# Four tokens in a row on each partition, one transfer for a token shift, fewer half-blocks on GpSimd, and a new order of steps

## The reference, cut to what matters

```
def shift_token(t):
    t1, t2 = jnp.split(t, 2, axis=-1)
    t2 = jnp.pad(t2, ((0, 0), (1, 0), (0, 0)))[:, :-1]
    return jnp.concatenate([t1, t2], axis=-1)
```

```
h = shift_token(x);  q, k, v = split(h @ wqkv)     # 8 heads of 64, windows of 64 tokens
q, k = rotary(l2norm(q)), rotary(l2norm(k))
x = x + local_attention(q, k, v) @ wo
h = shift_token(x);  h = layernorm(h) @ w1 + b1    # 2 x 341 wide
a, g = split(h);  x = x + (a * gelu(g)) @ w2 + b2
```

## Time and profile before

| what | value |
|---|---|
| median of 3 runs | 1747.68 us (1747.63 to 1748.17) |
| the profiled execution, its own time | 1748.34 us |
| its span, first to last instruction | 1746.6 us |
| mean granted TensorE clock | 0.918 |
| busy: PE, DVE, ACT, POOL | 1430.4, 1347.3, 1446.5, 1269.3 us |

### The profile page before, as it was taken

How to read it: one execution, slowest core, us unless ns; L and a number is a source line. 1 busy time by engine, 2 the same in 40 slices (tenths; PEclk the granted TensorE clock), 3 DMA queues, 4 the chain that set the end, 5 groups by cost and what they waited for, 6 DMA issues and landing times.

```text
span 1746.6 us, 40282 instructions
## 1 busy us (share of the span) xinstructions
PE 1430.4 (82%) x14680; PEld 1149.1 (66%) x14680; DVE 1347.3 (77%) x2148; ACT 1446.5 (83%) x4046; POOL 1269.3 (73%) x1639
## 2 busy tenths in 40 slices
PE   1566888888889988888889988888898888787874
PEld 1455667676777776677777767676777766565663
DVE  4998588888788888888888988888889877547821
ACT  1456989998999989988989998998999888696981
POOL 2847687787777888777777877777778776566741
PEclk9587999998999989999999999999999889899987
DMA  4012212222221222222122222221222222112210
GB/s 144 5 39 34 47 31 55 62 49 54 45 51 42 36 64 43 54 57 54 39 45 53 36 65 44 54 57 44 49 44 45 41 49 44 32 36 52 45 40 18
DMA packets 234565, 83.03 MB, mean 48 GB/s; under 512 B 175189, under 2 KB 215426, under 8 KB 234370
## 3 DMA queue, kind: packets, MB, share of 16 engines
q1 hardware_dynamic: 233074, 79.91, 21.4%
q10 hardware_dynamic: 1296, 0.56, 0.1%
HBM read 17.54 MB, written 8.39 MB: 15 GB/s over the span
## 4 chain that ended last, share of the span: by engine, by line
ACT 31%; PE 21%; DVE 19%; SPq 15%; issue 7%; DMA 5%; POOL 3%; DVEq 0%; ACTq 0%; POOLq 0%
SPq L471 12%; ACT sb_pl L624 9%; DMA sb_hs<-sb_x 4%; ACT sb_pl L631 4%; PE banks L947 3%; DVE banks L748 3%; DVE sb_ssq L794 3%; ACT sb_hid L662 3%; PE banks L851 3%; PE banks L925 3%; ACT sb_gate L657 2%; PE banks L988 2%; ACT L657 2%; PE banks L852 2%; PE banks L853 2%
## 5 line engine op out<-in xcount | busy, mean ns | idle before, releaser
L624 ACT ACTIVATE sb_pl<-banks,sb_nml,sb_rn 128x128 f32<-128x128 f32 x1024 | 455.7, 478 | 13.5 <-POOL sb_nml L557 13.4
L534 POOL TENSOR_TENSOR sb_qk<-sb_qk,sb_t 128x1024 f32<-128x1024 f32 x128 | 302.9, 2366 | 13.8 <-DVE sb_t L784 13.8
L529 POOL TENSOR_TENSOR sb_pr<-sb_qkvf 128x2048 f32<-128x2048 f32 x64 | 292.0, 4562 | 4.1 <-DVE banks L748 4.1
L947 PE MATMUL banks<-sb_pT,sb_vs 128*64 128x64 f32 x2048 | 149.0, 244 | 114.9 <-ACT sb_v L577 104.0
L851 PE MATMUL banks<-sb_wqh,sb_hh 128*128 128x512 f32 x384 | 184.2, 480 | 58.6 <-DVE sb_t L784 35.5
L624 ACT ACTIVATION_READ_ACCUMULATOR sb_pl<-banks,sb_nml,sb_rn 128x1 f32 x1024 | 231.4, 226 | 0.0
L947 PEld LDWEIGHTS banks<-sb_pT,sb_vs 128*64 128x64 f32 x2048 | 115.7, 152 | 147.6 <-ACT sb_v L577 112.3
L799 DVE TENSOR_REDUCE sb_nmx<-banks 128x4 f32<-128x512 f32 x256 | 163.7, 680 | 56.7 <-PE banks L925 56.7
L601 ACT ACTIVATE sb_sq<-banks 128x1024 f32<-128x1024 f32 x128 | 134.2, 1049 | 56.5 <-PE banks L853 56.0
L816 DVE BATCH_NORM_STATS2 sb_st<-sb_hs 128x6 f32<-128x128 f32 x128 | 27.9, 281 | 184.6 <-DMA sb_hs<-sb_x 184.6
L779 DVE TENSOR_TENSOR sb_qk<-banks,sb_tab 128x1024 f32<-128x1024 f32 x128 | 155.1, 1212 | 18.0 <-ACT sb_sq L601 17.4
(11 more groups left out here) (119 smaller groups left out, 4042.8 us busy)
## 6 DMA issues: line engine op xcount, KB each, us to landing
sb_vs<-sb_v SPq DMA_DIRECT2D x224, 128.0 KB, 2.3
sb_xt<-x SPq DMA_DIRECT2D x16, 256.0 KB, 3.3
sb_hh<-sb_sh SPq DMA_DIRECT2D x32, 128.0 KB, 2.7
sb_hl<-sb_sl SPq DMA_DIRECT2D x32, 128.0 KB, 2.4
heads_scratch<-sb_ofs SPq DMA_DIRECT2D x64, 64.0 KB, 3.3
sb_hs<-sb_x SPq DMA_DIRECT2D x32, 128.0 KB
sb_ob<-x SPq DMA_DIRECT2D x16, 256.0 KB, 3.2
sb_orow<-heads_scratch SPq DMA_DIRECT2D x16, 256.0 KB, 3.2
```

What stands on the lines that cost most here:

```text
L529: nc.gpsimd.tensor_tensor(pr[:].rearrange("p (q k d) -> p q k d", q=H, k=H), q[:, :, None, :].to_broadcast([P, H, H, D]), k[:, None, :, :] ...
L534: nc.gpsimd.tensor_tensor(qk[:, k, :], qk[:, k, :], t2[:, TURN[step] % 2, :], ALU.add).then_inc(s_add.sem, 1)
L624: last = nc.scalar.activation(pl[:, k, m, :], ps[:, m * P:(m + 1) * P], ACT.Exp, bias=nml[:, k, m:m + 1], scale=rn[:, TURN[step] // 2 % RN ...
L947: last = mm(ps[h * LD:(h + 1) * LD, pair * P + w * WIN:pair * P + (w + 1) * WIN], vals[:, n, head * LD:(head + 1) * LD], pT[:, turn, pair, ...
```

## The change

- **Layout.** x is loaded (and the output stored) with tokens 4p to 4p + 3 on partition p. `x1` and `x2` get a fifth block in front, whose second half holds the token before the partition's first. The rows of the weights that meet shifted features are rolled by 64 on the host, so that "second half of block b - 1, first half of block b" is one contiguous run of 128 elements, `shifted(buffer, b)`. `bn_stats`, `norm2` and the transposes of `x1` read that run; `hs` is gone.
- **Transfers.** `shift_x2` is one transfer from 127 partitions to the next, one run of 64 elements each. Layer 1's `shift_x` (four transfers after the split) becomes `shift_x1`, one such transfer ahead of `x1_t`, and `x1_split` and `x1_low` write `hh` and `hl` directly. `hh`, `hl` have three sides in place of two. Layer 0 keeps its four transfers.
- **Order of tokens.** The copies out of PSUM that must put tokens back in order read it with a step: `x_split`, `x1_split` (ACT) and `x_low`, `x1_low` (DVE) take every 128th element, `o_copy` (ACT) every fourth.
- **Half-blocks.** `POOL_SCALED` has three entries in place of four.
- **Chains.** `stats` gives up its aggregates to a step `aggr`, `stats2` to `aggr2`; `full_scores` becomes `full_scores`, `full_max`, `full_less`; `full_values` becomes `full_values`, `full_out`, `full_norm`. The instructions are the same; each part has its own slot.
- **Order.** All slots, and the places of the first and last units, are new.

```
-POOL_SCALED = (1, 3, 5, 7)
+POOL_SCALED = (1, 4, 6)
...
-    "o_copy": (235.13, 246.54, 254.87, 258.78), "out_local": (263.78,), "x2": (266.56,), "shift_x2": (267.90,),
-    "stats2": (272.42,), "rstd2": (277.08,), "norm2": (278.33,), "norm2_t": (280.96,), "high2": (282.03,), "low2": (285.29,),
+    "out_local": (227.5112,), "x2": (230.4382,), "shift_x2": (233.0435,), "stats2": (235.6252,), "aggr2": (236.6378,),
+    "rstd2": (237.6456,), "norm2": (242.9309,), "norm2_t": (244.3596,), "high2": (245.4327,), "low2": (245.7646,),
...
-    "x1": (303.91,), "x1_t": (305.37,), "x1_split": (305.91,), "x1_low": (306.78,),
+    "shift_x": (117.3139,), "x1": (269.0942,), "shift_x1": (276.6645,), "x1_t": (276.8388,), "x1_split": (278.5542,),
+    "x1_low": (280.0510,),
...
+SIDE = {unit: n % 3 for n, unit in enumerate(step[1:3] for step in KIND["project_qk"] if step[3] == 0)}
...
-        x1 = sb("x1", [P, 3, NB, E])
+        x1 = sb("x1", [P, 3, NB + 1, E])
-        hh, hl = sb("hh", [P, 2, S], F32R), sb("hl", [P, 2, S], F32R)
+        hh, hl = sb("hh", [P, 3, S], F32R), sb("hl", [P, 3, S], F32R)
-        x2, hs, hn = sb("x2", [P, 2, NB, E]), sb("hs", [P, NB, E]), sb("hn", [P, NB, E])
+        x2, hn = sb("x2", [P, 2, NB + 1, E]), sb("hn", [P, NB, E])
+        def shifted(buffer, b):
+            return buffer.rearrange("p n e -> p (n e)")[:, b * E + E // 2:(b + 1) * E + E // 2]
+        def token_order(ps):
+            return ps.rearrange("e (b p) -> e p b", b=NB)
+        def by_token(rows):
+            return rows.rearrange("e (p b) -> e p b", b=NB)
...
-        x_rows = t["x"].rearrange("s (n p) e -> s p n e", p=P)
+        x_rows = t["x"].rearrange("s (p n) e -> s p n e", p=P)
...
                 if kind == "shift_x":
-                    for dst, src in ((hh, sh[l]), (hl, sl[l])):
-                        sp.dma_start(dst[0:64, k, :].bitcast(F32), src[0:64, :].bitcast(F32)).then_inc(s_shift[k].sem, 16)
-                        sp.dma_start(dst[64:128, k, 1:S].bitcast(F32), src[64:128, 0:S - 1].bitcast(F32)).then_inc(s_shift[k].sem, 16)
+                    for dst, src in ((hh, sh), (hl, sl)):
+                        sp.dma_start(dst[0:64, u, 1:S].bitcast(F32), src[64:128, 0:S - 1].bitcast(F32)).then_inc(s_shift[k].sem, 16)
+                        sp.dma_start(dst[64:128, u, :].bitcast(F32), src[0:64, :].bitcast(F32)).then_inc(s_shift[k].sem, 16)
+                if kind == "shift_x1":
+                    sp.wait_ge(s_x1.sem, s_x1.at(("x1", s, 0, 0), step))
+                    sp.dma_start(x1[1:P, s % 3, 0, E // 2:E], x1[0:P - 1, s % 3, NB, E // 2:E]).then_inc(s_xs.sem, 16)
...
                 if kind == "shift_x2":
                     k = TURN[step] % 2
                     sp.wait_ge(s_x2.sem, s_x2.at(same("x2", step, 0), step))
-                    if before(step):
-                        sp.wait_ge(s_n2.sem, s_n2.at(("norm2", *before(step)[1:]), step))
-                    sp.dma_start(hs[1:P, :, 64:128], x2[0:P - 1, k, :, 64:128]).then_inc(s_hs.sem, 16)
-                    sp.dma_start(hs[0:1, 1:NB, 64:128], x2[P - 1:P, k, 0:NB - 1, 64:128]).then_inc(s_hs.sem, 16)
-                    sp.dma_start(hs[:, :, 0:64], x2[:, k, :, 0:64]).then_inc(s_hs.sem, 16)
+                    sp.dma_start(x2[1:P, k, 0, E // 2:E], x2[0:P - 1, k, NB, E // 2:E]).then_inc(s_hs.sem, 16)
...
-                    copy(sh[0][:], ps).then_inc(s_xhigh.sem, 1)
+                    copy(by_token(sh[:]), token_order(ps)).then_inc(s_xhigh.sem, 1)
...
-                    copy(oTl[:, :, n * P:(n + 1) * P], bank(same("values", step, n)).rearrange("p (a c) -> p a c", a=NPAIR)).then_inc(s_oc.sem, 1)
+                    q = P // NB
+                    copy(oTl[:, :, :].rearrange("p a (b q) -> p a b q", b=NB)[:, :, :, n * q:(n + 1) * q],
+                         bank(same("values", step, n)).rearrange("p (a q b) -> p a b q", a=NPAIR, b=NB)).then_inc(s_oc.sem, 1)
...
-                    copy(sh[1][:], ps).then_inc(s_x1h.sem, 1)
+                    user = in_unit_before("project_v", ("project_v", s, 1, 0), NB - 1, 3)
+                    act.wait_ge(s_v.sem, s_v.at(user, step))
+                    copy(by_token(hh[:, SIDE[s, 1], :]), token_order(ps)).then_inc(s_x1h.sem, 1)
...
                 if kind == "stats2":
                     dve.wait_ge(s_hs.sem, s_hs.at(same("shift_x2", step, 0), step))
                     for b in range(NB):
-                        last = nc.vector.bn_stats(st2[:, b, :], hs[:, b, :])
+                        last = nc.vector.bn_stats(st2[:, b, :], shifted(x2[:, TURN["x2", s, l, 0] % 2, :, :], b))
                     last.then_inc(s_bn2.sem, 1)
-                    dve.wait_ge(s_bn2.sem, s_bn2.at(step, step))
+                if kind == "aggr2":
+                    dve.wait_ge(s_bn2.sem, s_bn2.at(same("stats2", step, 0), step))
...
                 if kind == "x1_t":
                     claim(step)
-                    pe.wait_ge(s_x1.sem, s_x1.at(same("x1", step, 0), step))
-                    for b in range(NB):
-                        last = nc.tensor.transpose(ps[:, b * P:(b + 1) * P], x1[:, s % 3, b, :], ident[:])
+                    pe.wait_ge(s_xs.sem, s_xs.at(("shift_x1", s, 0, 0), step))
+                    for b in range(NB):
+                        last = nc.tensor.transpose(ps[:, b * P:(b + 1) * P], shifted(x1[:, s % 3, :, :], b), ident[:])
...
+    for name, axis in (("wqkv", 1), ("w1", 1), ("ln_g", 1), ("ln_b", 1)):
+        arrays[name] = np.roll(np.asarray(arrays[name]), E // 2, axis=axis)
```

More of the change, by code:

```diff
@@ L50 @@
+HEADS_SCALE = (0.5958681, 1.1193597, 0.7838495, 1.0049087, 1.0274403)
 UNIT_SLOTS = {
[L51 to L60, removed]
@@ L66 @@
-    "hid": (291.62, 296.02, 296.17), "down": (298.99,),
+    "project_qk": (133.2706, 140.6019, 155.8009, 164.0772), "square": (134.7374, 143.9946, 157.3681, 166.6953),
+    "rope": (140.5400, 148.3686, 159.5946, 178.7506), "ssq": (140.8325, 146.2960, 164.0333, 171.1343),
+    "rope_add": (142.1987, 160.2711, 167.5196, 183.2775), "rnorm": (149.8376, 176.7697),
+    "normed": (154.4511, 162.8918, 182.9419, 183.7601), "project_v": (159.0725, 181.4664, 186.1013, 186.6209),
+    "v_copy": (159.9898, 183.8122, 188.2271, 189.9351), "move_v": (168.5510, 184.9583, 202.4625, 215.3760),
@@ L298, in build @@
         s_bn = signal("block_stats", "stats")
-        s_stats = signal("stats_done", "stats")
+        s_stats = signal("stats_done", "aggr")
         s_rstd = signal("rstd_steps", "rstd1", 3)
@@ L433, in _ @@
                 if kind == "shift_x":
-                    k = TURN[step] % 2
-                    last = (low[l], ("x_low" if l == 0 else "x1_low", s, 0, 0))
-                    sp.wait_ge(last[0].sem, last[0].at(last[1], step))
-                    user = in_unit_before("project_v", step, NB - 1, 2)
+                    k, u = TURN[step] % 2, SIDE[s, 0]
+                    sp.wait_ge(s_xlow.sem, s_xlow.at(("x_low", s, 0, 0), step))
+                    user = in_unit_before("project_v", step, NB - 1, 3)
                     if user:
@@ L514, in _ @@
                 if kind == "rstd1":
-                    pool.wait_ge(s_stats.sem, s_stats.at(("stats", s, 0, 0), step))
+                    pool.wait_ge(s_stats.sem, s_stats.at(("aggr", s, 0, 0), step))
                     if s:
@@ L563, in _ @@
                 if kind == "rstd2":
-                    pool.wait_ge(s_st2.sem, s_st2.at(same("stats2", step, 0), step))
+                    pool.wait_ge(s_st2.sem, s_st2.at(same("aggr2", step, 0), step))
                     if before(step):
@@ L726, in _ @@
                     dve.wait_ge(s_load[s % 3].sem, s_load[s % 3].at(("load", s, 0, 0), step))
+                    if s >= 2:
+                        in_order(("aggr", s - 2, 0, 0), step)
                     for b in range(NB):
@@ L729, in _ @@
                     last.then_inc(s_bn.sem, 1)
-                    dve.wait_ge(s_bn.sem, s_bn.at(step, step))
+                if kind == "aggr":
+                    dve.wait_ge(s_bn.sem, s_bn.at(("stats", s, 0, 0), step))
                     if s:
```

138 lines of the change are left out of this document (79 added, 59 removed).

## The result

The changed kernel takes 1642.2 us (median of 4 runs, 1640.4 to 1642.8), the kernel before on the same chip 1747.7. The profiled execution took 1640.42 us, its span is 1638.6.

The account below looks back on a forecast made before the run. It took the slow 6.5 us issue of the second shift, on every unit's chain, as the bound, with ScalarE fullest. Start -5, middle -35 and end -14 sum to -54 from 1748.3: 1694 us, own range 1675 to 1718.

Parts of the forecast that it names:

- the mechanism of the shift: Second shift: one 127-partition transfer replaces three, taking 4.1 us in place of 9.85; waits at `norm2` and `values` go.
- start, to the third shift: First stage: two shifts with idle engines around them, -11 us, and +6 for VectorE's new order: -5 us.
- middle, 23 units: The 23 middle units: ScalarE's work 46.5 plus waits 1.7 gives 48.2 us each, -1.5 per unit, -35 us.
- end: Last units: -5.7 us in the last, half of it in five others, +6 for ScalarE's extra work: -14 us.
- the count for `norm2`: ScalarE's list up to `norm2`, 15.2 us, against 13.1 until its input is ready: wait gone, margin about 1 us.
- Two shifts: Start: two second shifts with idle engines around them, each 5.7 us shorter, -11 us.
- +6 for the full part: Start: more full-part work and other sequences' `stats` and `aggr` on VectorE ahead of the third `x2`, half charged: +6 us.
- The half-block's +6: End: the half-block moved to ScalarE adds 1.3 us in each of five units, +6 us.
- Rival 1: ScalarE nearly full, only `o_copy`'s 0.5 us wait left: 47.1 us per unit, 1669 us, or 1655; chance 0.18.
- Rival 2: Another wait replaces `norm2`'s on ScalarE, idle time stays 4.5 us: 51.0 us per unit, 1759 us; chance 0.08.
- Rival 3: Copies reading PSUM with a step cost 0.61 us more each, five per unit: +98, 1792 us; chance 0.04.
- Rival 4: The shift doesn't get shorter, 127 partitions being slow whatever their runs; ScalarE's 41 us stay: 1789 us; chance 0.02.

Follow-up runs that it names:

- e4: The kernel before, with the L470 transfer from 127 partitions cut into two of 112 and 15; 1626.5 us, ratio 0.932.
- e3: The changed kernel with four half-blocks (1, 3, 5, 7) on GpSimd in place of three (1, 4, 6); 1646.6 us, ratio 0.943.
- e9: The changed kernel with two half-blocks (1, 6) on GpSimd in place of three; 1678.5 us, ratio 0.960.
- e11: e1 with layer 1's first shift as in the kernel before: x1 transposed unshifted, split, then moved by four transfers; 1631.3 us, ratio 0.930.
- e1: The changed kernel's new layout with the slots, places and half-blocks of the kernel before, split chain parts placed back to back; 1656.9 us, ratio 0.949.
- e6: The changed kernel with each part of a split chain placed right behind its head again; 1697.0 us, ratio 0.970.

## Why the prediction was right or wrong

**Right: the mechanism of the shift.** The one transfer is issued in 0.65 us, the shift takes 3.44 us (forecast 4.1), the waits at `norm2` and in front of `values` are gone, the copies with a step cost nothing, GpSimd is down 32 us (33). e4 shows, by one cut transfer, that the form of L470 (127 partitions) was the cause; that it ran through one engine rests on the DMA share of 0.08.

**Wrong: the size.** Against the spans, 1746.6 and 1638.6:

| term | forecast | measured |
|---|---|---|
| start, to the third shift | -5 | -7.2 |
| middle, 23 units | -35 | -80.0 |
| end | -14 | -20.8 |
| sum | -54 | -108.0 |

The step that failed is in the middle's term: "ScalarE's work 45.2 + 1.3 = 46.5; its waits ... 1.7 in all: 48.2". It is 45.79 + 0.45 = 46.24. Of the 2.0 us, 1.2 are the half-block (0.05 in place of 1.29, from e3 to the change), 0.6 the waits and 0.35 the work with the issue gone and nothing else (e4: 1.10 and 44.88); layout and order, which no term had there, took 0.2 back (46.19 in e3 against 45.99 in e4). It failed in three ways.

- *Other waits of the same stall.* Only `norm2`'s was taken as going in full, the square's by half, `high2`'s not at all. In e4, where only the issue changed, the square has 8.1 us left of 18.5, `high2` 1.5 of 13.6, `o_copy` all of its 12.2, and ScalarE's idle time is 1.10 us per unit. So a good part of the short waits on other lines was an echo of the one stall, but not every wait.
- *Work and waits added.* They needn't be independent: from e3 to the change ScalarE has 0.90 us more work and 0.85 us less idle time. The half-block cost the unit 0.05 us, not 1.29 (with the reservation above, that the half-blocks are also others). Only the next (e9) costs in full. The forecast should have been the larger of "ScalarE's work and a little" and "the chain", not the sum.
- *Prices from an engine that stalls.* Durations overlap, and busy time depends on the stalls; why it does isn't shown. The same 2914 instructions are busy for 45.2 us a unit before and 44.9 in e4. In ScalarE's timeline of the changed kernel four scales follow each other in 1.17 us, where the sum used 1.29. A copy takes 0.48 from start to start, where the count for `norm2` used 0.61:

```profile
758.87 1.35 ACT L651 ACTIVATE sb_pl<-sb_pl,sb_rl 128x128 f32<-128x128 f32 x4
760.04 1.09 ACT L621 ACTIVATE sb_sq<-banks 128x1024 f32<-128x1024 f32 x1
760.95 0.67 ACT L597 ACTIVATE sb_kT<-banks 128x512 f32<-128x512 f32 x1
761.42 0.68 ACT L597 ACTIVATE sb_qT<-banks 128x512 f32<-128x512 f32 x1
761.90 0.48 ACT L693 ACTIVATE banks<-banks 128x256 f32<-128x256 f32 x1
```

ScalarE's busy time grew by 26 us, where 41 were forecast. In the 23 units it is 0.90 us per half-block from e3 to the change, and 0.36 us per unit less work before that, in e4.

**The start.** "Two shifts" at -5.7 and +6 for the full part gave -5 against -7.2. The number is near by luck. The last table splits it: the end of the issue alone gave 4.7 us there, not 11; the new layout in the old order lost 10.5, which no term had, at the transfer in front of `x1_t` (e11, without it, has the third shift 12 us earlier than e1); the new order and the run of the change gave back 13. The forecast called the transfer hidden by nine us of other work. In the changed kernel that holds, 4.5 us of waits in the whole run where e1 has 37.4. It also put SP's waits in front of `heads` at nothing; in e1 that place in SP's list holds the transfer back by 5.7 us.

**The end.** -20.8 against -14. With only the issue gone (e4) the end is 30 us shorter: the forecast took half a gain in five units, and in full it would have been 34. The half-block's +6 isn't seen (-1.3). Against that, layout and new order cost 11 us at the end, which no term had. So this near hit too is made of larger errors that cancel.

**The rivals.** Rival 1, ScalarE nearly full, was the right picture: its idle time is 0.45, it said 0.5 at `o_copy`. Its 1669 to 1655 was too high, mostly by the work's price. Rival 2, another wait in `norm2`'s place, didn't come; e6 shows a part of it, since with the chains joined ScalarE is idle for 2.06 us a unit in place of 0.45 and the kernel takes 1697, far from the rival's 1759. The split, which the forecast valued at nothing, is worth 55 us in the new order. The range's upper end of 1735 was called a forecast with a third of rival 2 in it; a third of their 65 us gives 1716. Rival 3, stepped reads, is refuted by the copies of the changed kernel in the 23 units, `o_copy` (stepped, oTl) against three without a step, mean ns of one ahead of the idle time:

```profile
L597 ACT ACTIVATE sb_kT<-banks 128x512 f32<-128x512 f32 x92 | 63.1, 686 | 0.0
L597 ACT ACTIVATE sb_qT<-banks 128x512 f32<-128x512 f32 x92 | 62.6, 681 | 0.0
L597 ACT ACTIVATE sb_v<-banks 128x512 f32<-128x512 f32 x92 | 62.3, 677 | 0.0
L597 ACT ACTIVATE sb_oTl<-banks 128x512 f32<-128x512 f32 x92 | 56.7, 688 | 8.6 <-PE banks L983 8.6
```

All four are longer than the 612 ns of the earlier trace rows, stepped or not. In one and the same order, without a step (e4) and with it (e1), `o_copy` takes:

```profile
L578 ACT ACTIVATE sb_oTl<-banks 128x512 f32<-128x512 f32 x128 | 80.2, 630 | 15.0 <-PE banks L948 14.9
```

```profile
L594 ACT ACTIVATE sb_oTl<-banks 128x512 f32<-128x512 f32 x128 | 79.9, 627 | 19.6 <-PE banks L980 19.6
```

The rule of the Trainium skill (Advanced Engine Details and Errata, section "Memory Cachelines") isn't borne out for ScalarE's copies with a step of four elements; its sentence is on matmuls. Rival 4 is out with the 3.44 us.

**Where the 105 us come from**, in steps that were each run. The first two columns are medians. The last three are differences within the profiled executions, up to the third shift, from there to the twenty-sixth, and from there to the end:

| step | us | total | start | middle | end |
|---|---|---|---|---|---|
| before | | 1747.7 | | | |
| the 6.5 us issue gone, old layout and order (e4) | -121 | 1626.5 | -4.7 | -85.9 | -30.2 |
| new layout in the old order (e1) | +30 | 1656.9 | +10.5 | +11.6 | +2.8 |
| new order, chains split (e3) | -10 | 1646.6 | -7.3 | -6.9 | +7.9 |
| three on GpSimd (the change) | -4 | 1642.2 | -5.6 | +1.1 | -1.3 |

The last step is not clear of noise. The order of the steps is a choice: joined chains cost 55 us in the new order, and the slow issue 243. What stays open is what holds e3's unit at 46.2 us; its ScalarE waits are all short (10.1 us in 23 at `o_copy` the largest), and none was taken away by itself.

## What to carry to other kernels

Cut a large transfer from 127 partitions into one of 112 and one of 15, before anything is laid out anew: one transfer cut in two gave 121 us here. When a stall on every unit's chain is removed, forecast the next bound as the larger of the fullest engine's work, priced from starts in a back-to-back stretch, and the next chain; part of the waits elsewhere is an echo of the stall and goes with it. Then share the work out again: the share that the kernel had under the stall (four of eight) isn't the best without it (five). And look at what stands ahead of a new transfer in its queue's list, not only at how long it takes.
